# Results of the experts added in memory by the scatters of an MoE layer, after a differential attention and before and after a decaying attention

## Chip, cores and metric

One Trainium2 chip (trn2), one core. The metric is the device time of one execution in microseconds (us), median of 3 runs. TensorE is called PE below, VectorE DVE, ScalarE ACT, GpSimd POOL, SyncE SP. PE's clock has two levels, 1.2 and 2.4 GHz, and the profile gives the granted clock as a share of the upper one.

## What is computed

The input `x` holds 2 x 1024 tokens of 128 numbers. Four layers follow each other, each added to the residual; the second and the fourth are the same mixture of experts with the same weights:

```python
x = x + diff_attention(layernorm(x))      # 16 heads of 8
x = x + ffn(layernorm(x))                 # "m1" below
x = x + decay_attention(layernorm(x))     # 16 heads of 64
x = x + ffn(layernorm(x))                 # "m2" below

def ffn(x):
    scores = softmax(xf @ router_w.T)     # 8 experts
    topk_scores, topk_ids = top_k(scores, 2)
    topk_scores = topk_scores / topk_scores.sum(-1, keepdims=True)
    # each token: sum over its 2 experts of
    # score * ((silu(x @ w_gate) * (x @ w_up)) @ w_down), FF = 512
```

With two chosen experts the normalized scores are 1 / (1 + e) and e / (1 + e), where e is the exponential of the difference of the two logits.

## The kernel before

The residual `X` stays in SBUF as 128 partitions x 16 tiles x 128. `program` calls `diff_attention`, `moe` with tag m1, `decay_attention`, `moe` with tag m2, and the store of the output. Each is a block in which every engine has its own list of instructions in program order, tied by semaphores; blocks are separated by a barrier.

**In diff_attention** SP holds a list over 16 groups of heads (L533 to L549): `m_store(g)` stores the maxima of a group, and `load_operands(g + 2, ...)` loads the queries and keys of the group after next from DRAM, 24 transfers, once the second pass of PE is done with the group whose slot they take. PE computes the maxima of the groups ahead of the second pass; a transpose `turn` (L565) ends those of one group and those of the next begin.

**In moe** the routing comes first. PE counts tokens per expert (L1224, L1226) into `RC`, DVE turns the counts into places (`over` L1454 to `placeb` L1473), builds one-hot matrices in four passes over `c` (`marks`, `place_oh`, L1478 to L1483), and PE multiplies them into `IV`, from which DVE makes two lists: `source`, the token of each row, and `target`, the row where its result goes (L1494 to L1507). A slot is 128 rows for one expert; there are 39 slots, and 39 x 128 rows hold the 4096 results and some empty rows. ACT meanwhile normalizes `X` into `XN` (L1348), SP stores it as `xn_rows` in DRAM in four quarters (L1158). DVE takes the difference of the two best logits (`far`, L1485, L1486), ACT its exponential (L1351), which needs another table of functions, and then loads the table for Silu (L1354).

Then come the slots. POOL has this list: eight gathers ahead (L1196, `xs`, eight buffers), then for each slot s one gather for slot s + 8 and the scatter of slot s (L1202), which waits until DVE has copied the result from PSUM to `ys` (L1524, four buffers). PE turns a gathered tile (L1247), multiplies gate and up (L1256) and down (L1265); ACT copies weights (L1368) and takes Silu (L1362); DVE multiplies gate and up (L1517). The scatter writes first choices to rows 0 to 2047 of `yd_rows` and second choices to rows 2048 to 4095, and empty rows behind them.

Behind the slots `results_in` (L1147 to L1151) waits for all scatters, and SP and ACT load the first and the second results in four quarters each (`GB`, `gathered[q][k]`). ACT multiplies each tile of second results by its weight (`weigh`, L1387, 4 x 128x128 a quarter); DVE adds weight times first result to `X` (L1552, 4 x 128x128) and then the weighted second results (L1558, one of 128x512). In m1 the quarter goes on: statistics and mean (L1535, L1538) on DVE, the deviation on ACT (`deviations`, L1392), reciprocal and shift on DVE (`scales`, L1543, L1544), the normalized rows on ACT (`rows`, L1398), a transpose on PE and its copy on ACT (`turned_copy`, L1403). The last quarter's rows are made on DVE (L1568). PE runs products that nobody reads (L1300) in the waits: 26, then two for each weighed tile. In m2 SP stores the output in quarters (L2285), from the moment that the last quarter of first results has landed.

The constants of a layer are written by POOL at its start (L1178 to L1190); DVE waits for all eight of them (`const_r`) before `over`.

## Time and profile before

| what | value |
|---|---|
| median of 3 runs | 1128.02 us (1126.24 to 1129.11) |
| profiled execution: its time / its span | 1128.58 / 1126.8 us |
| PE, DVE, ACT, POOL busy | 1013.5, 749.7, 749.4, 438.6 us |
| granted clock of PE, mean | 0.956 |
| HBM read / written | 47.86 / 14.68 MB |

The span is the time from the first to the last instruction, and the execution's own time is 1.8 us more. Busy times are sums over layers that are bound by different things. m1 lies from about 492 to 653 us of the span, m2 from about 977 to the end.

### The profile page before, as it was taken

Reading aid. Unit: us, or ns where it says so; the run is one execution under the profiler, and the core shown is the slowest. Engines: PE = TensorE matmul, PEld = TensorE weight load, DVE = VectorE, ACT = ScalarE, POOL = GpSimd, SP = SyncE. Lnnn points to the kernel's source line nnn. Section 1 sums busy time; section 2 is a strip of 40 time slices with the busy share of each in tenths; the row PEclk is TensorE's granted clock in tenths of the full one; section 3 lists DMA queues with packets and bytes.
Section 4 is the critical chain, followed back from the end, with each engine's and each line's share of the span. In section 5 each row is a group of like instructions: output and inputs, shape, how many; then the busy total and the mean of one; then the engine's idle time right before and its main releaser. Section 6 shows DMA issues by size and latency. Waiting matters only on the chain. (4 is left out here: it accounts for less than half of the span.)

```text
span 1126.8 us, 26278 instructions
## 1 busy us (share of the span) xinstructions
PE 1013.5 (90%) x9920; PEld 696.6 (62%) x9920; DVE 749.7 (67%) x1513; ACT 749.4 (67%) x1513; POOL 438.6 (39%) x580
## 2 busy tenths in 40 slices
PE   5889999999999999758999889999999999489993
PEld 3333333333333334547999768787888888479993
DVE  6789999999999998882333545656565666443333
ACT  4658888888888887445666577675766666356663
POOL 3752112221121211216765134544444444257761
PEclk9889999999999999978999899999999999779997
DMA  2233111111111100611111421111111110021114
GB/s 71 88 111 114 31 30 43 46 31 30 30 36 45 39 2 2 222 41 46 48 48 37 160 71 76 38 76 38 77 38 76 39 74 3 10 62 50 48 41 126
DMA packets 40035, 64.67 MB, mean 57 GB/s; under 512 B 10025, under 2 KB 21033, under 8 KB 37993
## 3 DMA queue, kind: packets, MB, share of 16 engines
q1 hardware_dynamic: 31736, 50.14, 13.9%
q0 software_dynamic: 4992, 10.23, 3.4%
q10 hardware_dynamic: 3184, 2.63, 0.7%
q8 instruction: 82, 1.34, 0.5%
q14 instruction: 41, 0.33, 0.1%
HBM read 47.86 MB, written 14.68 MB: 56 GB/s over the span
## 5 line engine op out<-in xcount | busy, mean ns | idle before, releaser
L802 ACT ACTIVATE PB<-S 128x512 f32<-128x512 f32 x576 | 307.9, 597 | 71.0 <-PE S L608 66.2
L908 DVE TENSOR_REDUCE mx<-S 128x2 f32<-128x1024 f32 (+1 forms) x192 | 207.5, 1127 | 8.5 <-PE S L594 8.5
L870 POOL TENSOR_SCALAR_AFFINE_SELECT PB<-PB 128x512 f32<-128x512 f32 x128 | 79.3, 638 | 306.4 <-ACT PB L802 306.3
L643 PE MATMUL PV<-PB,VP 128*32 128x256 f32 (+2 forms) x2432 | 177.7, 379 | 0.0
L1517 DVE TENSOR_TENSOR m_hs<-m_gs,m_UP 128x512 f32<-128x512 f32 x78 | 53.7, 688 | 158.7 <-ACT m_gs L1362 156.6
L608 PE MATMUL S<-W 50*128 50x512 bf16 (+3 forms) x768 | 123.9, 328 | 4.9 <-ACT PB L802 4.2
L594 PE MATMUL S<-W 48*128 48x512 bf16 (+3 forms) x640 | 94.4, 326 | 13.1 <-DVE mx L904 4.9
L1202 POOL DMA_INDIRECT yd_rows<-m_ys,m_target x78 | 76.8, 984 | 58.9 <-DVE m_ys L1524 58.9
L1196 POOL DMA_INDIRECT m_xs<-xn_rows,m_source x78 | 76.0, 974 | 48.0 <-DVE m_source L1497 24.8
L643 PEld LDWEIGHTS PV<-PB,VP 128*32 128x32 f32 x2432 | 51.6, 108 | 69.1 <-issue 59.4
L594 PEld LDWEIGHTS S<-W 48*128 48x128 bf16 x640 | 26.8, 94 | 108.4 <-issue 43.1
L1256 PE MATMUL m_GP<-m_xt,m_wgu 128*128 128x128 f32 x624 | 84.5, 279 | 1.8 <-ACT m_xt L1358 1.8
L898 DVE TENSOR_REDUCE mx<-S 128x8 f32<-128x1024 f32 x64 | 78.3, 1223 | 10.8 <-PE S L587 10.1
L1256 PE MATMUL m_UP<-m_xt,m_wgu 128*128 128x128 f32 x624 | 83.9, 278 | 0.0
L1265 PE MATMUL m_YP<-W,m_hs 128*128 x624 | 82.6, 275 | 1.2 <-DVE m_ys L1524 1.2
L1368 ACT ACTIVATE m_wgu<-W 128x1024 f32 x78 | 82.6, 1058 | 1.4 <-issue 1.3
L1358 ACT ACTIVATE m_xt<-m_XT 128x128 f32<-128x128 f32 x78 | 21.7, 278 | 90.8 <-PE m_XT L1247 90.8
L1890 ACT ACTIVATE d_enegs<-d_PA 128x512 f32<-128x512 f32 x64 | 37.8, 591 | 64.7 <-PE d_PA L1684 60.2
L1256 PEld LDWEIGHTS m_GP<-m_xt,m_wgu 128*128 128x128 f32 x624 | 77.5, 195 | 2.9 <-issue 2.9
L1923 ACT ACTIVATE d_DM<-d_LQ,d_nL 128x128 f32<-128x128 f32 x252 | 78.1, 388 | 0.0
L1256 PEld LDWEIGHTS m_UP<-m_xt,m_wgu 128*128 128x128 f32 x624 | 77.6, 195 | 0.0
L1265 PEld LDWEIGHTS m_YP<-W,m_hs 128*128 128x128 f32 x624 | 75.8, 192 | 1.6 <-issue 1.6
(315 smaller groups left out, 1970.9 us busy)
## 6 DMA issues: line engine op xcount, KB each, us to landing
d_LQ<-l_rows SPq DMA_DIRECT2D x15, 1024.0 KB, 4.6
W<-qk_parts SPq DMA_DIRECT2D x210, 32.0 KB
qk_parts<-OT SPq DMA_DIRECT2D x24, 256.0 KB, 3.0
W<-qk_parts SPq DMA_DIRECT2D x30, 96.0 KB
W<-in_L_ffn_w_gate SPq DMA_DIRECT2D x1, 2048.0 KB, 10.0
W<-in_L_ffn_w_up SPq DMA_DIRECT2D x1, 2048.0 KB, 15.0
xn_rows<-m_XN SPq DMA_DIRECT2D x8, 256.0 KB, 2.3
m_GB<-yd_rows SPq DMA_DIRECT2D x8, 256.0 KB, 6.7
```

Source lines behind the costliest of these rows:

```text
L594: ins = nc.tensor.matmul(S1[:, b, a, 256 * k:256 * k + w], QS[base:base + KR, s, h, qb * P:(qb + 1) * P], KS[base:base + KR, s, h, c * 512 ...
L608: ins = nc.tensor.matmul(S2[:, j % 3, col:end], KS[base:base + KM, s, h, kb * P:(kb + 1) * P], QS[base:base + KM, s, h, q0:q0 + end - col] ...
L643: ins = nc.tensor.matmul(PV[32 * u:32 * u + 32, shift + col:shift + end], VP[:, g, kb, u // 2, :], PB[:, slot, col:end], start=(kb == 0 an ...
L802: nc.scalar.activation(PB[:, j % NPB, :], S2[:, j % 3, :], ACT.Exp, scale=SC).then_inc(exp_done, 1)
L870: nc.gpsimd.affine_select(out=tri, in_=tri, compare_op=ALU.is_ge, fill=0.0, base=0, pattern=[[0, U], [1, P]], channel_multiplier=-1).then_ ...
L898: nc.vector.reduce_max(mx[:, g % 2, 2].rearrange("p a h q -> p (a h) q")[:, :, q:q + 2], S1[:, b].rearrange("p a (h j k) -> p (a h) j k", ...
L908: nc.vector.reduce_max(mx[:, g % 2, c, :, heads[0], qb], S1[:, b, :, 0:w], AX.X)\
L1202: pool.indirect_dma_start(out=YD[:, :], out_offset=bass.IndirectOffsetOnAxis(ap=target[:, s:s + 1], axis=0), in_=ys[:, s % YB], in_offset= ...
L1256: last = nc.tensor.matmul(H[:, s % 2, j * P:(j + 1) * P], wgu[:, s % 2, k, j * P:(j + 1) * P], xt[:, s % 2], start=True, stop=True)
L1265: last = nc.tensor.matmul(YP[:, 0:P], hs[:, s % 2, j * P:(j + 1) * P], WD[:, bass.ds(e, 1), j, :].rearrange("p o d -> p (o d)"), start=(j ...
L1368: nc.scalar.activation(wgu[:, s % 2], W3[:, 0:2 * n].rearrange("p (k e f) -> p k e f", k=2, e=E) [:, :, bass.ds(e, 1), :].rearrange("p k o ...
L1923: last = nc.scalar.activation(DM[:, i, j % 2, j // 2], LQ[:, b, h], ACT.Exp, bias=nL[:, t, h:h + 1])
```

## The change

The weights of the choices are now in the table that is gathered: a row of `XN` and `xn_rows` has 130 numbers, the last two being 1 / (1 + e) and e. DVE takes a slot's weight from the gathered rows (`weight(s)`), and the copy out of PSUM multiplies by it. Each layer has its own result table. SP stores `X` into its first 2048 rows at the start of the layer, and SP writes zeros (7040 rows of 512 B) to all rows behind them during diff_attention, behind `m_store(2)` for m1 and `m_store(3)` for m2. The scatters add in memory (`compute_op=ALU.add`). Behind the slots one sum of the two loaded rows gives `X`; `weigh`, L1552 and the tile `wts` are gone. For this the exponential is taken ahead of `XN`: POOL computes `far`, ACT loads the table for Exp behind the first deviation, and the first quarter of `XN` is stored once the two extra columns are there. DVE waits for two constants before `over` and for all eight before `slotb`; in m2 it makes `rstd` and `shift` before the counts.

```diff
                     for g in range(1, G):
                         m_store(g)
+                        if g in (2, 3):
+                            clear_results(sp, "m1" if g == 2 else "m2")
...
-    XD, YD = scratch["xn"], scratch["yd"]
+    XD, YD = scratch["xn"], scratch["yd"][tag]
...
+        RW = P + 2
+        XNW = sb("XN", [P, NT, RW])
+        XN = XNW[:, :, 0:P]
...
             def _(sp):
+
+                sp.dma_start(YD[0:NTOK, :].rearrange("(p t) d -> p t d", t=NT), X[:]).then_inc(x_stored, 16)
                 for q in range(NQ):
                     sp.wait_ge(xn_ready, TQ * q + TQ)
-                    sp.dma_start(XD[q * TQ * P:(q + 1) * TQ * P, :].rearrange("(t p) d -> p t d", p=P), XN[:, quarter(q), :])\
+                    if q == 0:
+                        sp.wait_ge(table_ready, 1)
+                    sp.dma_start(XD[q * TQ * P:(q + 1) * TQ * P, :].rearrange("(t p) d -> p t d", p=P), XNW[:, quarter(q), :])\
...
                         pool.wait_ge(xt_done, s - XB + 1)
+                        pool.wait_ge(row_weighted, s - XB + 1)
...
                     pool.indirect_dma_start(out=YD[:, :], out_offset=bass.IndirectOffsetOnAxis(
-                        ap=target[:, s:s + 1], axis=0), in_=ys[:, s % YB], in_offset=None)\
+                        ap=target[:, s:s + 1], axis=0), in_=ys[:, s % YB], in_offset=None, compute_op=ALU.add)\
                         .then_inc(ys_stored[s % YB], 16)
 
+
+                nc.gpsimd.tensor_tensor(far[:], top[:, :, 1], top[:, :, 0], ALU.subtract).then_inc(apart, 1)
+                pool.wait_ge(apart, 1)
+                pool.wait_ge(rstd_ready, 1)
+                nc.gpsimd.tensor_tensor(far[:], far[:], rstd[:], ALU.mult).then_inc(far_ready, 1)
...
                 pool.wait_ge(targeted, 1)
+                pool.wait_ge(x_stored, 16)
+                pool.wait_ge(scratch["yd_zeroed"], 32)
                 for s in range(SLOTS):
                     if s + XB < SLOTS:
...
                     unread_products(26)
-                    for t in range(NT):
-                        pe.wait_ge(weighted, t + 1)
-                        unread_products(2)
+                    for q in range(NQ):
+                        pe.wait_ge(gathered[q][0], 16)
+                        unread_products(4)
...
                 nc.scalar.activation(sd[:, deviations_done:], mv[:, deviations_done:, 1], ACT.Sqrt, bias=norm["eps"][:])\
                   .then_inc(sd_ready, 1)
+
+                nc.scalar.activation(unread[:], norm["eps"][:], ACT.Exp)
+                act.wait_ge(far_ready, 1)
+                nc.scalar.activation(far_exp[:], far[:], ACT.Exp).then_inc(far_exp_ready, 1)
                 act.wait_ge(shift_ready, 1)
                 for t in range(NT):
                     nc.scalar.activation(XN[:, t, :], X[:, t, :], ACT.Identity, scale=rstd[:, t:t + 1],
                                          bias=shift[:, t:t + 1]).then_inc(xn_ready, 1)
-                act.wait_ge(far_ready, 1)
-                nc.scalar.activation(far_exp[:], far[:], ACT.Exp).then_inc(far_exp_ready, 1)
 
...
-                    for q in range(NQ):
-                        weigh(q)
...
-                    weigh(0)
-                    weigh(1)
-                    weigh(2)
                     deviations(0)
-                    weigh(3)
                     rows(0)
...
+                def scale():
+                    dve.wait_ge(sd_ready, 1)
+                    nc.vector.reciprocal(rstd[:], sd[:]).then_inc(rstd_ready, 1)
+                    dve.wait_ge(rstd_ready, 1)
+                    nc.vector.scalar_tensor_tensor(out=shift[:], in0=mv[:, :, 0], scalar=-1.0, in1=rstd[:], op0=ALU.mult,
+                                                   op1=ALU.mult).then_inc(shift_ready, 1)
+
+                if statistics_done == NT:
+                    scale()
+
+
                 dve.wait_ge(rc_done, 1)
-                dve.wait_ge(const_r, NCONST)
+                dve.wait_ge(const_r, 2)
                 total = RC[:, NT * E:(NT + 1) * E]
                 chain.link(nc.vector.tensor_tensor(over[:], total.unsqueeze(2).to_broadcast([P, E, NT]),
                                                    iot[:].unsqueeze(1).to_broadcast([P, E, NT]), ALU.is_gt))
                 chain.link(nc.vector.reduce_sum(tiles[:], over[:], AX.X))
-                dve.wait_ge(sd_ready, 1)
-                chain.link(nc.vector.reciprocal(rstd[:], sd[:]))
-                nc.vector.scalar_tensor_tensor(out=shift[:], in0=mv[:, :, 0], scalar=-1.0, in1=rstd[:], op0=ALU.mult,
-                                               op1=ALU.mult).then_inc(shift_ready, 1)
+                if statistics_done < NT:
+                    scale()
...
+                dve.wait_ge(const_r, NCONST)
                 nc.vector.tensor_copy(slotb[:].rearrange("p c i -> p (c i)"), sloti[:])
...
-                chain.link(nc.vector.tensor_tensor(far[:], top[:, :, 1], top[:, :, 0], ALU.subtract))
-                nc.vector.tensor_tensor(far[:], far[:], rstd[:], ALU.mult).then_inc(far_ready, 1)
+                    if m == 0:
+
+                        dve.wait_ge(far_exp_ready, 1)
+                        chain.link(nc.vector.tensor_scalar_add(far_sum[:], far_exp[:], 1.0))
+                        nc.vector.reciprocal(XNW[:, :, P], far_sum[:])
+                        nc.vector.tensor_copy(XNW[:, :, P + 1], far_exp[:]).then_inc(table_ready, 1)
...
-                dve.wait_ge(far_exp_ready, 1)
-                chain.link(nc.vector.tensor_scalar_add(far_sum[:], far_exp[:], 1.0))
-                chain.link(nc.vector.reciprocal(wts[:, 0], far_sum[:]))
-                chain.link(nc.vector.tensor_tensor(wts[:, 1], far_exp[:], wts[:, 0], ALU.mult))
+                chain.link(nc.vector.tensor_scalar(first_choice[:], iv[:, 2], -1.0, 1.0, ALU.mult, ALU.add))
+
+
+                def weight(s):
+                    dve.wait_ge(xs_loaded[s % XB], s // XB * 16 + 16)
+                    nc.vector.scalar_tensor_tensor(out=row_weight[:, s:s + 1], in0=xs[:, s % XB, P + 1:P + 2],
+                                                   scalar=first_choice[:, s:s + 1], in1=xs[:, s % XB, P:P + 1],
+                                                   op0=ALU.max, op1=ALU.mult).then_inc(row_weighted, 1)
...
-                    nc.vector.tensor_copy(ys[:, s % YB], YP[:, 0:P]).then_inc(y_copied, 1)
+                    dve.wait_ge(row_weighted, s + 1)
+                    nc.vector.tensor_scalar(ys[:, s % YB], YP[:, 0:P], row_weight[:, s:s + 1], None, ALU.mult).then_inc(y_copied, 1)
 
                 for s in range(SLOTS):
+                    weight(s)
                     gate(s)
                     if s:
                         y_copy(s - 1)
...
                     dve.wait_ge(xn_ready, NT)
                 for q in range(NQ):
                     dve.wait_ge(gathered[q][0], 16)
-                    for t in range(TQ * q, TQ * q + TQ):
-                        last = nc.vector.scalar_tensor_tensor(out=X[:, t, :], in0=GB[:, q, 0, t % TQ],
-                                                              scalar=wts[:, 0, t:t + 1], in1=X[:, t, :], op0=ALU.mult,
-                                                              op1=ALU.add)
-                    last.then_inc(first_added, 1)
-                    dve.wait_ge(weighted, TQ * q + TQ)
-                    dve.wait_ge(first_added, q + 1)
-                    nc.vector.tensor_tensor(X[:, quarter(q), :], X[:, quarter(q), :], GB[:, q, 1], ALU.add)\
+                    dve.wait_ge(gathered[q][1], 16)
+                    nc.vector.tensor_tensor(X[:, quarter(q), :], GB[:, q, 0], GB[:, q, 1], ALU.add)\
                       .then_inc(summed, 1)
                     if follow is not None:
...
+        def clear_results(sp, tag):
+            rows = scratch["yd"][tag][NT * P:, :].rearrange("(p k) d -> p k d", p=P)
+            sp.wait_ge(zeros_set, 1)
+            sp.dma_start(rows, zeros[:].unsqueeze(1).to_broadcast([P, NT + Router.SLOTS, P])).then_inc(yd_zeroed, 16)
```

How the instructions of three engines stand at three places, in program order; `x4` is a run of four, and line numbers with the change are those of the changed file. Start of m2 on ACT, before (L1344 is the deviation, `m_unread` a result that nobody reads, there to load a table):

```order
L1344 ACTIVATE norm_sd<-norm_mv,norm_eps 128x2
L1348 ACTIVATE m_XN<-X,m_shift,m_rstd 128x128 x16
L1351 ACT_TABLE_LOAD
L1351 ACTIVATE m_far_exp<-m_far 128x16
L1354 ACT_TABLE_LOAD
L1354 ACTIVATE m_unread<-m_far_exp 128x1
```

and with the change:

```order
L1361 ACTIVATE norm_sd<-norm_mv,norm_eps 128x2
L1364 ACT_TABLE_LOAD
L1364 ACTIVATE m_unread<-norm_eps 128x1
L1366 ACTIVATE m_far_exp<-m_far 128x16
L1369 ACTIVATE m_XN<-X,m_shift,m_rstd 128x128 x16
L1373 ACT_TABLE_LOAD
L1373 ACTIVATE m_unread<-m_far_exp 128x1
```

The exponential and its table stand ahead of the sixteen rows of `XN` instead of behind them.

DVE in m2, before: the end of the last of the four one-hot passes and what follows it.

```order
L1482 TENSOR_SCALAR m_marks<-m_marks,m_iop 128x312
L1483 TENSOR_TENSOR m_place_oh<-m_lane_no,m_placeb 128x1024
L1485 TENSOR_TENSOR m_far<-route_top 128x16
L1486 TENSOR_TENSOR m_far<-m_far,m_rstd 128x16
L1488 TENSOR_TENSOR m_sover<-m_ios,m_ends 1x312
L1490 TENSOR_REDUCE m_sef<-m_sover 1x39
L1491 TENSOR_SCALAR m_etab<-m_sef 1x39
```

With the change, DVE from the first pass to the second:

```order
L1495 TENSOR_TENSOR m_marks<-m_slot_no,m_slotb 128x312
L1497 TENSOR_TENSOR m_marks<-m_marks,m_tile_no 128x312
L1499 TENSOR_SCALAR m_marks<-m_marks,m_iop 128x312
L1500 TENSOR_TENSOR m_place_oh<-m_lane_no,m_placeb 128x1024
L1505 TENSOR_SCALAR m_far_sum<-m_far_exp 128x16
L1506 RECIPROCAL m_XN<-m_far_sum 128x16
L1507 COPY m_XN<-m_far_exp 128x16
L1495 TENSOR_TENSOR m_marks<-m_slot_no,m_slotb 128x312
L1497 TENSOR_TENSOR m_marks<-m_marks,m_tile_no 128x312
```

The three instructions of the table's columns (L1505 to L1507) stand between the first and the second pass, and the two of `far` are gone from DVE.

End of m1 on ACT, before (`m_GB` is the loaded results, `d_XNT` the copy of the turned rows):

```order
L1387 ACTIVATE m_GB<-m_GB,m_wts 128x128 x12
L1392 ACTIVATE norm_sd<-norm_mv,norm_eps 128x4
L1387 ACTIVATE m_GB<-m_GB,m_wts 128x128 x4
L1398 ACTIVATE m_XN<-X,m_shift,m_rstd 128x128 x4
L1392 ACTIVATE norm_sd<-norm_mv,norm_eps 128x4
L1398 ACTIVATE m_XN<-X,m_shift,m_rstd 128x128 x4
L1403 ACTIVATE d_XNT<-m_GP 128x512
L1392 ACTIVATE norm_sd<-norm_mv,norm_eps 128x4
L1398 ACTIVATE m_XN<-X,m_shift,m_rstd 128x128 x4
L1403 ACTIVATE d_XNT<-m_GP 128x512
L1392 ACTIVATE norm_sd<-norm_mv,norm_eps 128x4
L1403 ACTIVATE d_XNT<-m_GP 128x512 x2
```

and with the change:

```order
L1405 ACTIVATE norm_sd<-norm_mv,norm_eps 128x4
L1411 ACTIVATE m_XN<-X,m_shift,m_rstd 128x128 x4
L1405 ACTIVATE norm_sd<-norm_mv,norm_eps 128x4
L1411 ACTIVATE m_XN<-X,m_shift,m_rstd 128x128 x4
L1416 ACTIVATE d_XNT<-m_GP 128x512
L1405 ACTIVATE norm_sd<-norm_mv,norm_eps 128x4
L1411 ACTIVATE m_XN<-X,m_shift,m_rstd 128x128 x4
L1416 ACTIVATE d_XNT<-m_GP 128x512
L1405 ACTIVATE norm_sd<-norm_mv,norm_eps 128x4
L1416 ACTIVATE d_XNT<-m_GP 128x512 x2
```

The sixteen multiplications L1387 are gone, and the rest keeps its order.

## Rows read from the trace of the kernel before

**Rows 1.** The chain of waits over the whole execution, shares by engine and line
```profile
by line: PE m_GP L1256 3.2%; PE m_UP L1256 3.1%; PE m_YP L1265 3.0%; DMA m_GB<-yd_rows 0.6%; PE m_UP L1237 0.5%; PE m_XT L1247 0.4%; issue 0.3%; DMA m_xs<-xn_rows,m_source 0.2%; DMA yd_rows<-m_ys,m_target 0.2%; ACT m_GB L1387 0.1%; POOL m_l
```

**Rows 2.** Timeline of POOL in the slots of m2 (start us, us, engine, line, what, idle before)
```profile
1051.57 0.98 POOL L1196 DMA_INDIRECT m_xs<-xn_rows,m_source  x1 [0.30 <-issue]
1053.07 0.98 POOL L1202 DMA_INDIRECT yd_rows<-m_ys,m_target  x1 [0.52 <-DVE m_ys L1524]
1054.36 0.98 POOL L1196 DMA_INDIRECT m_xs<-xn_rows,m_source  x1 [0.30 <-issue]
```

**Rows 3.** DMA issues by line: count, median us from issue to landing
```profile
m_xs<-xn_rows,m_source POOLq DMA_INDIRECT x78, 2.6
yd_rows<-m_ys,m_target POOLq DMA_INDIRECT x78, 2.3
```

**Rows 4.** Timeline of the end of m1, all engines
```profile
633.17 0.69 DVE L1558 TENSOR_TENSOR X<-X,m_GB 128x512 f32<-128x512 f32 x1 [0.41 <-ACT m_GB L1387]
...
635.26 1.28 ACT L1387 ACTIVATE m_GB<-m_GB,m_wts 128x128 f32<-128x128 f32 x4 [2.12 <-DMA m_GB<-yd_rows]
...
637.86 0.33 SPq L2270 DMA_DIRECT2D d_WK<-in_L_attn_b_Wk  x1
637.98 0.28 ACT L1392 ACTIVATE norm_sd<-norm_mv,norm_eps 128x4 f32<-128x4 f32 x1
...
643.57 0.57 ACT L1403 ACTIVATE d_XNT<-m_GP 128x512 f32<-128x512 f32 x1
...
644.91 0.17 DVE L1543 RECIPROCAL m_rstd<-norm_sd 128x4 f32<-128x4 f32 x1
...
645.31 1.65 ACT L1398 ACTIVATE m_XN<-X,m_shift,m_rstd 128x128 f32<-128x128 f32 x4 [0.98 <-DVE m_shift L1544]
...
647.66 0.18 DVE L1543 RECIPROCAL m_rstd<-norm_sd 128x4 f32<-128x4 f32 x1 [1.18 <-ACT norm_sd L1392]
```

**Rows 5.** Timeline of the end of m2, all engines
```profile
1109.98 0.97 POOL L1202 DMA_INDIRECT yd_rows<-m_ys,m_target  x1 [0.78 <-DVE m_ys L1524]
...
1119.85 2.54 ACT L1387 ACTIVATE m_GB<-m_GB,m_wts 128x128 f32<-128x128 f32 x8 [0.68 <-DMA m_GB<-yd_rows]
...
1120.93 3.58 SPq L2285 DMA_DIRECT2D out_x<-X  x4
...
1123.41 0.69 DVE L1558 TENSOR_TENSOR X<-X,m_GB 128x512 f32<-128x512 f32 x1
```

**Rows 6.** Timeline of the start of m2, all engines
```profile
977.80 0.30 ACT L1344 ACTIVATE norm_sd<-norm_mv,norm_eps 128x2 f32<-128x2 f32 x1 [5.71 <-PEq L2281]
...
979.81 0.17 PE L1226 MATMUL m_UP<-route_M,m_tri 128*128 128x8 bf16 x1
...
981.37 0.29 DVE L1454 TENSOR_TENSOR m_over<-m_UP,m_iot 128x128 f32<-128x128 f32 x1 [4.57 <-POOL m_spare L1175]
...
982.01 0.25 DVE L1458 RECIPROCAL m_rstd<-norm_sd 128x16 f32<-128x16 f32 x1
...
993.49 0.17 DVE L1510 TENSOR_SCALAR m_far_sum<-m_far_exp 128x16 f32<-128x16 f32 x1
...
993.72 1.05 POOL L1196 DMA_INDIRECT m_xs<-xn_rows,m_source  x1 [12.46 <-DVE m_source L1497]
993.98 0.17 DVE L1512 TENSOR_TENSOR m_wts<-m_far_exp,m_wts 128x16 f32<-128x16 f32 x1
```

**Rows 7.** Timeline of the start of m1, DVE
```profile
496.03 0.29 DVE L1454 TENSOR_TENSOR m_over<-m_UP,m_iot 128x128 f32<-128x128 f32 x1 [0.68 <-POOL m_spare L1175]
```

**Rows 8.** The SyncE queue's timeline in attention, groups 2 and 3
```profile
118.98 2.44 SPq L529 DMA_DIRECT2D W<-mrow  x4
124.48 1.99 SPq L111 DMA_DIRECT2D W<-qk_parts  x6
```

**Rows 9.** Timeline of PE at the end of group 3's maxima
```profile
141.00 0.28 PE L565 MATMUL S<-ident,mxc 128*32 128x128 f32 x1
```

**Rows 10.** Stretch in which m1 stores XN: busy, PEclk, DMA share, GB/s
```profile
500.00:504.00 4.00, 3.16 (x15) 2.23 (x16) 3.90 (x12) 3.98 (x10) 0.00 (x0) 0.50 0.64 180
```

More of the change, by code:

```diff
@@ L1139, in moe @@
         ZP = XT[:, 0:NT * HE]
-        YTS = xs[:].rearrange("p b d -> p (b d)")
+        YTS = wgu[:, 0].rearrange("p k f -> p (k f)")
         NCONST = 8
@@ L2238, in _ @@
                 nc.gpsimd.memset(identb[:], 0.0).then_inc(ident_zero, 1)
+                nc.gpsimd.memset(zeros[:], 0.0).then_inc(zeros_set, 1)
                 nc.gpsimd.memset(norm["eps"][:], LN_EPS)
```

30 lines of the change are left out of this document (14 added, 16 removed).

## Prediction

> **What bounds the kernel.** I read the chain of waits first. It says which engine holds the end: PE in m2's slots (L1256, L1265) has most of what the answer covers, and two smaller entries bear on this change, the loads of results into `GB` (0.6%) and the two kinds of indirect transfers (0.2% each) [rows 1]. The slots are PE's: gathers start 2.79 us apart (1054.36 less 1051.57) all along, and only what lengthens that period, or what stands before and behind the 39 slots of a layer, can move the time. POOL is nearly full in a slot: a gather and a scatter, each 0.98 us with 0.30 us behind it, make 2.56 of 2.79 us, so 0.23 us are left [rows 2]. Then the timelines of four places: the two ends and the two starts of the MoE layers. Behind m1's slots, ACT and DVE work through quarters; the last quarter's reciprocal starts at 647.66 [rows 4], and all of decay_attention is behind it. Behind m2's slots the last quarter of results is there by 1121, while the last sum starts at 1123.41 [rows 5]. At m2's start DVE is idle for 4.57 us until POOL has written its last constant, and the first gather waits for DVE's list [rows 6].
>
> **End of m1.** Gone are 16 multiplications on ACT and 16 multiply-adds on DVE; the sum of a quarter (0.69 us) stays. What is late next? The second quarter is there at 635.26 (ACT's wait for it ends) and the last by 637.86, when SP, which waits for it, issues the next load [rows 4]. With the change the chain from 635.26 is: the sum, 0.69, and reciprocal with shift, 0.40 (644.91 to 645.31), so that ACT starts the rows of quarter 0 at 636.4. From there ACT and DVE alternate: three times rows of 1.65, three times a deviation of 0.28 and the 0.40 again (the last without the rows), and twice a copy of 0.57: 4.95 + 0.84 + 0.80 + 1.14 = 7.7, with some 0.05 for each of eight handoffs 8.1. The last reciprocal starts at 644.5 instead of 647.66: **-3.2 us**. DVE's sums and statistics (about 2.0 us a quarter) lie beside it, and the third and fourth quarters land before they are needed. What follows is unchanged work, if PE's clock holds.
>
> **End of m2.** ACT's last multiplications are released by a landing at 1119.85 and last 2.54 us for two quarters, so the last quarter has landed by 1121.1. One sum of 0.69 then ends at 1121.85, where it now ends at 1124.10. SP cannot start storing before 1120.93 in either kernel, and its 3.58 us for four stores hold waits for sums [rows 5]. Without them four issues of some 0.45 us end near 1122.6 instead of 1124.5: **-1.9 us**.
>
> **Start of m2.** DVE is released by the last matmul of the counts (979.81 + 0.17) instead of the last constant (981.37): -1.3. The reciprocal and what hangs on it (0.25 and its gap) go into the idle time behind the deviation of 977.80: -0.3. The two-column work comes in between the first and the second one-hot pass. The same three operations took from 993.49 to 994.15 before: +0.66. The first gather at 993.72 waited for DVE's `source`: **-1.0 us** [rows 6]. The rows of `XN` don't become the later wait: ACT's table load now stands in its idle time, the exponential is released by POOL behind its constants at about 981.75, and `XN` starts 0.4 us earlier than before; only its first quarter is stored 1 us later, behind the columns, and it isn't the last.
>
> **Start of m1.** The idle time before `over` is only 0.68 [rows 7], the columns cost 0.66, and the reciprocal stays in the chain: 0. `XN` starts about 0.3 us later behind the table load, and it has that room before the list.
>
> **In the slots.** `weight(s)` is one tiny DVE operation, and the copy becomes a multiplication, perhaps 0.05 us longer. DVE has nearly 2 us of each slot free, so 38 of 39 cost nothing; if the copy grew by over half a microsecond, PE would wait for it. The last one of a layer is exposed, as is one memset at the very start: +0.2 together.
>
> **The adding scatter** is in no row. Two prices. *Landing*: a plain scatter lands in 2.3 us, a gather, which reads DRAM, in 2.6 [rows 3]. Adding means reading the row, then writing. Lower bound 0, upper bound a whole gather in front, +2.6. Only the last scatter of a layer is exposed. I take +0.8, nearer to the low end, since the issue and completion inside those 2.6 are paid once; two layers: **+1.6 us**. The Trainium skill ("DMA: Bandwidth & Descriptors", Latency and other measured facts) gives an HBM access of 0.2 us on average; by that the term would be an estimated 0.4 and the sum 1.2 us lower. No row here shows it. *Issue on POOL*: lower bound 0, upper bound a second 0.98. I take +0.3, which exceeds the 0.23 us of slack by so little that four `ys` buffers absorb it (next part).
>
> **Traffic that is added.** SP writes 2 x 7040 rows of 512 B, 3.6 MB each, ahead of the loads of groups 4 and 5. The store of 512 B rows moved 180 GB/s at a DMA share of 0.64 [rows 10], so 280 GB/s at full share: 12.8 us. It starts when `m_store(2)` is issued (118.98 + 2.44 = 121.4), and is through by about 135.5. The loads that were issued from 124.48 land some 3 us behind it, near 139 [rows 8]. PE needs them when the maxima of group 3 are done, at 141.00 [rows 9]: hidden, with 2 to 3 us to spare, and the same pattern 23 us later for m2. The store of `X` (1 MB) lies ahead of the first `XN` store with 6 us of idle DMA. Rows of 520 B instead of 512 B: 0.
>
> **The sum.** -3.2 - 1.9 - 1.0 + 0.2 + 1.6 = -4.3. The profiled execution took 1128.58 us for a span of 1126.8; 1124.3 for one like it. The median of the runs is 0.56 lower, which gives **1123.7 us**, 0.4% below 1128.02. A measurement of this kernel can tell about 0.3% (3.4 us) from no change, so the line for faster is 1124.6.
>
> **Rivals.**
> - *POOL becomes the bound (slower).* If an adding scatter takes d longer to issue, POOL falls behind by d - 0.23 in each of the 31 slots that also have a gather. DVE needs the `ys` buffer four slots later: 4 x 2.79 = 11.2, less copy and handoff (0.6) and landing (3.1), leaves 7.5 us of lag, so it decides from d = 0.23 + 7.5 / 31 = 0.47. Above it each layer loses 31 x (d - 0.47); at d = 0.7 that is 7.1 us a layer and **1138 us**. At double the issue it would be 1155. For it: POOL's 0.98 us is the making of a list of transfers, and adding needs a second source. Against it: gather and scatter cost the same, though they differ in direction. A rule of the Trainium skill bears on it ("DMA: Bandwidth & Descriptors", SDMA does more than copy, and SWDGE vs HWDGE vs iDMA): addition there takes two streams, and POOL writes a descriptor pair for each copied row. Three descriptors instead of two would be an estimated d = 0.49, at the edge, and the time 1125.
> - *The gain is given back at the ends (no change).* Either the added read costs its upper bound (+3.6 more, 1127.3), or PE, which now has 16 unread products instead of 32 behind m1's slots and ACT's rows come in quarters between them, is at 1.2 GHz for the last transposes and the first products of decay_attention, which would return 2 to 3 us: about **1127 us**.
> - *Attention waits for its loads.* If writing zeros runs at the measured 180 GB/s instead of 280, it lasts 20 us, and the loads of groups 4 and 5 land near 144.5, 3.5 us late, twice: **1130.7 us**.
> - *The change does less than it says.* If the loads into `GB` land later, since four scatters that add are behind them in the memory, the quarters and not ACT set the end of m1; the saving then shrinks by as much. This is within the second case.
>
> **Chances.** Forecast 0.55 (of it 0.47 faster, 0.08 just short of the line, own range 1120.5 to 1126). Given back at the ends 0.19 (0.17 same, 0.02 slower). POOL 0.16 (0.03 same, 0.13 slower). Loads late 0.10, slower. Together faster 0.47, same 0.28, slower 0.25. The range reaches down to 1120, where landing costs nothing and the starts give a little more, and up to 1132, which holds late loads and a POOL bound of d up to 0.6; beyond it lies most of the POOL case, near 0.1, and some 0.05 lie below.
>
> **What the profile will show.** Right: POOL's scatter at most 1.4 us, gathers still 2.79 us apart in both layers, last reciprocal of m1 about 3 us earlier against the last scatter, one DVE operation of 0.69 per quarter in m2's end, `over` released by PE in m2, and no wait of PE for `qk_parts`. Wrong: DVE's multiplication waiting for `yd_rows`, a longer slot, a scatter landing beyond 4 us, or a granted clock below 1.00 from m1's last transposes on.

## The result, and the profile after the change

The changed kernel takes **1142.03 us** (median of 6 runs, 1140.07 to 1144.81), the kernel before 1128.57 us beside it (6 runs): ratio 1.0127, 95% interval 1.0108 to 1.0147. (The ratios here are taken over the fast runs and can differ a little from those of the medians, here 1.0119.) The prediction, 1123.7 us with a range of 1120 to 1132, was wrong in sign. The profiled execution took 1143.47 us for a span of 1141.6, so it is set against the 1126.8 of before: +14.8 us.

The table sets the same events of both traces side by side (start times in us, offset after less before). A stage costs what its offset has more than that of the line above.

| event | before | after | offset | the stage's own share |
|---|---|---|---|---|
| m1 begins (POOL's first fill) | 492.47 | 499.59 | +7.1 | attention **+7.1** |
| first gather of m1 | 508.45 | 514.89 | +6.4 | start -0.7 |
| last scatter of m1 | 625.04 | 638.51 | +13.5 | slots **+7.0** |
| loads into `GB` issued | 627.41 | 641.89 | +14.5 | last scatter **+1.0** |
| decay attention's first copy | 654.09 | 663.17 | +9.1 | end of m1 **-5.4** |
| m2 begins | 977.79 | 986.79 | +9.0 | decay attention -0.1 |
| first gather of m2 | 993.72 | 1001.41 | +7.7 | start -1.3 |
| last scatter of m2 | 1109.98 | 1124.00 | +14.0 | slots **+6.3** |
| loads into `GB` issued | 1112.35 | 1127.37 | +15.0 | last scatter **+1.0** |
| end of the span | 1126.8 | 1141.6 | +14.8 | end of m2 -0.2 |

Two things, the adding scatters and the place of the zeros, stand in the stages that cost 22 us, and the gains return 8.

**Slots.** The first fence is the timeline of POOL in m2 after the change, three scatters and two gathers in the middle and the last two (start us, us, engine, line, what, idle before). It answers to [rows 2].

```profile
1093.23 1.58 POOL L1212 DMA_INDIRECT yd_rows_m<-m_ys,m_target  x1 [0.30 <-issue]
1095.12 0.98 POOL L1206 DMA_INDIRECT m_xs<-xn_rows,m_source  x1 [0.31 <-issue]
1096.40 1.59 POOL L1212 DMA_INDIRECT yd_rows_m<-m_ys,m_target  x1 [0.30 <-issue]
1098.30 0.99 POOL L1206 DMA_INDIRECT m_xs<-xn_rows,m_source  x1 [0.30 <-issue]
1099.59 1.58 POOL L1212 DMA_INDIRECT yd_rows_m<-m_ys,m_target  x1 [0.30 <-issue]
...
1122.15 1.55 POOL L1212 DMA_INDIRECT yd_rows_m<-m_ys,m_target  x1 [0.30 <-DVE m_ys L1550]
1124.00 1.55 POOL L1212 DMA_INDIRECT yd_rows_m<-m_ys,m_target  x1 [0.31 <-issue]
```

A gather still takes 0.98 us, the adding scatter 1.58 instead of 0.98. With 0.30 behind each the pair takes 3.17 us (1096.40 less 1093.23) where PE's slot took 2.79, and nothing but 0.30 stands before any row: POOL has become the bound. The last scatters, without gathers between them, are 1.85 apart. Who feels it is DVE, whose multiplication writes a buffer that a scatter must have left (the waits of the window 1000:1130):

```profile
DVE m_ys L1550 <- DMA yd_rows_m<-m_ys,m_target: 10.3, 12, 1.1
```

**Attention.** The queue of SP around the first transfer of zeros, after the change, against [rows 8]:

```profile
119.18 2.44 SPq L529 DMA_DIRECT2D W<-mrow  x4
121.66 0.60 SPq L2264 DMA_DIRECT2D yd_rows_m<-zeros  x1
124.69 11.10 SPq L111 DMA_DIRECT2D W<-qk_parts  x6
135.83 1.05 SPq L115 DMA_DIRECT2D W<-qk_parts  x3
136.92 2.00 SPq L111 DMA_DIRECT2D W<-qk_parts  x6
```

Then PE, where it ran out of work, against [rows 9]. First the same place in the kernel before:

```profile
140.00 0.29 PE L594 MATMUL S<-W 48*128 48x128 bf16 x4
...
140.43 0.64 PE L643 MATMUL PV<-PB,VP 128*32 128x256 f32 x8
```

and after the change:

```profile
143.17 0.40 PE L596 MATMUL S<-W 48*128 48x128 bf16 x4 [2.90 <-DMA W<-qk_parts]
...
143.92 1.08 PE L645 MATMUL PV<-PB,VP 128*32 128x256 f32 x8
144.93 0.40 PE L567 MATMUL S<-ident,mxc 128*32 128x128 f32 x1
```

The transfer of zeros itself is issued in 0.60 us. The six loads behind it (a group has 18, not 24) take 11.10 us to be issued, in place of 1.99, of which the first alone takes 8.35. PE then waits 2.90 us for `W<-qk_parts` with four products of the next group's first maxima, and those stand *ahead* of the turn that I had read as the moment of need (L565 before, L567 now, at 144.93). The wait has a second price: PE's granted clock, 1.00 before it and at this place of the kernel before, is 0.50 (the lower level) from 142.3 to 149.2 us. It falls near the end of the 2.90 us in which PE stands still, and then eight products of L645 take 1.08 us in place of 0.64. That costs another 2.6 us: the product that starts at 149.12 is 5.7 us later than in the kernel before (143.38), and 0.2 of these were there ahead of the zeros. The second transfer does it again without the clock: SP's loads take 10.05 us from 152.52, and PE waits 0.70 us at 169.43. The turn of that group is 6.25 us late (170.44, before 164.19), and the last turn, near 430 us, still 6.2. The remaining 0.9 of the 7.1 arises behind that turn, at the end of attention, where the clock is at the lower level for another 3.4 us from 483.6, before not at all; what releases it I did not trace. Run 1 gives all of it back. The zeros landed in 15.0 us (DMA issues by line, median from issue to landing):

```profile
yd_rows_m<-zeros SPq DMA_DIRECT2D x2, 3520.0 KB, 15.0
...
xn_rows<-m_XN SPq DMA_DIRECT2D x8, 260.0 KB, 4.0
```

**Starts and ends.** After the change the start of m2 reads, against [rows 6]:

```profile
989.01 0.29 DVE L1472 TENSOR_TENSOR m_over<-m_UP,m_iot 128x128 f32<-128x128 f32 x1 [1.42 <-PE m_UP L1243]
...
993.31 0.17 DVE L1505 TENSOR_SCALAR m_far_sum<-m_far_exp 128x16 f32<-128x16 f32 x1
...
993.51 0.26 DVE L1506 RECIPROCAL m_XN<-m_far_sum 128x16 f32<-128x16 f32 x1
993.68 0.12 DVE L1507 COPY m_XN<-m_far_exp 128x16 f32<-128x16 f32 x1
...
1000.05 0.18 DVE L1518 TENSOR_SCALAR m_source<-m_token 128x39 uint32<-128x39 f32 x1
...
1001.41 1.06 POOL L1206 DMA_INDIRECT m_xs<-xn_rows,m_source  x1 [10.51 <-DMA xn_rows<-m_XN]
```

`over` follows PE, as forecast. The first gather, though, waits no longer for the list (ready at 1000.23) but for the store of the rows, of which a quarter now lands in 4.0 us, in place of 2.3 with rows of 512 B. The end of m1, against [rows 4] (the sums and the last reciprocal):

```profile
641.89 1.75 SPq L1156 DMA_DIRECT2D m_GB<-yd_rows_m  x4
...
646.35 0.69 DVE L1579 TENSOR_TENSOR X<-m_GB 128x512 f32<-128x512 f32 x1 [9.74 <-DMA m_GB<-yd_rows_m]
...
648.28 0.66 DVE L1579 TENSOR_TENSOR X<-m_GB 128x512 f32<-128x512 f32 x1
...
650.34 0.66 DVE L1579 TENSOR_TENSOR X<-m_GB 128x512 f32<-128x512 f32 x1
...
652.62 0.66 DVE L1579 TENSOR_TENSOR X<-m_GB 128x512 f32<-128x512 f32 x1
...
656.65 0.18 DVE L1570 RECIPROCAL m_rstd<-norm_sd 128x4 f32<-128x4 f32 x1 [1.19 <-ACT norm_sd L1405]
```

And the end of m2, against [rows 5]:

```profile
1127.37 1.76 SPq L1156 DMA_DIRECT2D m_GB<-yd_rows_m  x4
...
1131.78 0.69 DVE L1579 TENSOR_TENSOR X<-m_GB 128x512 f32<-128x512 f32 x1 [9.66 <-DMA m_GB<-yd_rows_m]
1133.38 0.69 DVE L1579 TENSOR_TENSOR X<-m_GB 128x512 f32<-128x512 f32 x1 [0.91 <-DMA m_GB<-yd_rows_m]
1135.19 1.50 DVE L1579 TENSOR_TENSOR X<-m_GB 128x512 f32<-128x512 f32 x2 [1.12 <-DMA m_GB<-yd_rows_m]
1135.75 2.31 SPq L2318 DMA_DIRECT2D out_x<-X  x4
```

### The profile page after: what moved, and what is told of

Its sections match the earlier page's. It is cut to its first block and busy times, and to the rows that moved or that the text cites. A ratio compares the mean times of both kernels' runs of the same rounds, so it can differ in the third digit from the quotient of the medians.

```text
span 1141.6 us, 26345 instructions
## 1 busy us (share of the span) xinstructions
PE 1023.4 (90%) x9904; PEld 698.6 (61%) x9904; DVE 758.1 (66%) x1557; ACT 739.7 (65%) x1483; POOL 486.0 (43%) x585
## 3 DMA queue, kind: packets, MB, share of 16 engines
q0 software_dynamic: 13728, 10.31, 7.1%
## 5 line engine op out<-in xcount | busy, mean ns | idle before, releaser
L645 PE MATMUL PV<-PB,VP 128*32 128x256 f32 (+2 forms) x2432 | 179.7, 382 | 0.0
L1212 POOL DMA_INDIRECT yd_rows_m<-m_ys,m_target x78 | 123.4, 1582 | 26.2 <-issue 20.1
L645 PEld LDWEIGHTS PV<-PB,VP 128*32 128x32 f32 x2432 | 51.8, 109 | 70.6 <-issue 61.6
L1273 PE MATMUL m_GP<-m_xt,m_wgu 128*128 128x128 f32 x624 | 87.0, 284 | 1.8 <-ACT m_xt L1377 1.8
L1387 ACT ACTIVATE m_wgu<-W 128x1024 f32 x78 | 82.6, 1058 | 3.9 <-DVE m_etab L1512 2.6
## 6 DMA issues: line engine op xcount, KB each, us to landing
W<-in_L_ffn_w_up SPq DMA_DIRECT2D x1, 2048.0 KB, 15.1
```

The source lines that it names most:

```text
L645: ins = nc.tensor.matmul(PV[32 * u:32 * u + 32, shift + col:shift + end], VP[:, g, kb, u // 2, :], PB[:, slot, col:end], start=(kb == 0 an ...
L1212: pool.indirect_dma_start(out=YD[:, :], out_offset=bass.IndirectOffsetOnAxis(ap=target[:, s:s + 1], axis=0), in_=ys[:, s % YB], in_offset= ...
L1273: last = nc.tensor.matmul(H[:, s % 2, j * P:(j + 1) * P], wgu[:, s % 2, k, j * P:(j + 1) * P], xt[:, s % 2], start=True, stop=True)
L1387: nc.scalar.activation(wgu[:, s % 2], W3[:, 0:2 * n].rearrange("p (k e f) -> p k e f", k=2, e=E) [:, :, bass.ds(e, 1), :].rearrange("p k o ...
```

## The experiments

My first theory for the whole: *POOL's issue price* makes the slots' loss, *the place of the zeros on SP's queue* makes attention's, and the rest of the change gains. The rivals: the landing and four buffers (slots), the added bytes themselves (attention), the weight's operation on DVE (slots), and gains that existed only because the rest was slow. The kernels ran on three chips, each beside the kernel before. On the first chip the kernel before itself takes 1182 us (the last section has what its traces show), so three of the four kernels of that chip were run again on the second, where it takes 1127.89; on the third (runs 2, 7 and 8) it takes 1127.09. Run 4 ran on the first chip alone.

**Run 1: zeros in pieces.** In place of the two transfers, behind `load_operands`:

```diff
+                        if 2 <= g < 12:
+                            clear_results(sp, "m1" if g < 7 else "m2", (g - 2) % 5)
```

with `[:, 11 * piece:11 * piece + 11]` of the rows in each.

> The changed kernel (1142.0 us) with the zeros of both tables written in ten pieces of 704 KB, one behind the loads of each of the groups 4 to 13, in place of two transfers of 3520 KB that stand ahead of the loads of groups 4 and 5. Theory A: the 7 us that the attention lost came from the two bursts, which held back SP's next loads (11.1 and 10.1 us to issue in place of 2.0) and with them PE at 143 us; in pieces behind the loads nothing waits: the first layer starts at 492 to 493 us in place of 499.6, and the time is 1135, 1134 to 1136.5. Theory B: the 7 MB cost the same wherever they are written, or the attention lost time to something else (the memset, the planner's order): the start stays at 497 to 500, the time above 1139.

Measured 1142.96 us where before took 1181.99; m1 begins at 490.43. The begin speaks for theory A, the time says nothing on that chip. Again on another:

> The changed kernel with its zeros in ten pieces, a second time: 1135, 1134 to 1136.5, where the changed kernel takes 1142; on the first call's chip the first layer started at 490.4 us in place of 499.6, but the first scatter of a layer came 14.8 us after its first gather in place of 12.2. If the pieces cost the second half of the attention what the bursts cost the first, it is above 1139.

Measured **1135.20 us** (before 1127.89 beside it, ratio 1.0071, 1.0043 to 1.0098). m1 begins at 492.98. The 7 us of attention were the bursts; 7 MB of zeros in ten pieces cost nothing that can be seen, and no product waits for `W<-qk_parts`. POOL's first to last scatter stays at 110.5 us in both layers.

**Run 2: is it the size or the place?** The two transfers whole, moved behind `load_operands` in the loop of SP:

```diff
                         m_store(g)
-                        if g in (2, 3):
-                            clear_results(sp, "m1" if g == 2 else "m2")
...
                             load_operands(sp, g + 2, (g + 2) % NQ)
+                        if g in (2, 3):
+                            clear_results(sp, "m1" if g == 2 else "m2")
```

> The changed kernel with its two transfers of zeros whole, as the change has them, but issued behind the loads of groups 4 and 5 in place of ahead of them. Theory A: the 7 us were a matter of place: SP's next loads could not be issued for 9 us behind a transfer of 7040 rows, and PE waited for them; behind the loads nothing is due on SP for 11 us (131.0 to 142.2 us), the two tiles' loads have been issued, and the first layer starts at 492 to 494: the time is 1135, 1134 to 1137, as with the pieces. Theory B: 3.5 MB at once take the transfer engines from the loads of group 4, which have just been issued, so these land late and PE waits as before: start at 496 to 500, time 1139 to 1142.

Measured 1136.72 us (before 1127.09 beside it, ratio 1.0082, 1.0062 to 1.0103), m1 begins at 490.02. Theory A. That m1 begins earlier than in the kernel before (492.47) is no gain: PE's turn that stands at 118.04 us in the trace before is already 2.8 us earlier here, and no zeros are written yet; the later turns keep these 2.8 up to 400 us. SP's queue in that run:

```profile
121.70 1.98 SPq L111 DMA_DIRECT2D W<-qk_parts  x6
...
127.96 0.61 SPq L2264 DMA_DIRECT2D yd_rows_m<-zeros  x1
139.16 3.18 SPq L529 DMA_DIRECT2D W<-mrow  x4
```

The same 3520 KB are issued at 127.96, behind the loads; the next item is due 11 us later and takes 3.18 us in place of 2.41. The loads of group 4, issued just ahead, were not late: PE's list of waits has no entry for `W<-qk_parts` left.

**Run 3: scatters that overwrite.** `compute_op=ALU.add` is taken away, the zeros stay as the change has them. The kernel leaves out the addition, so the residual is missing from its sums.

> The changed kernel with scatters that overwrite in place of adding; zeros, the store of the residual, weights at the copies and the sum of two rows stay. It leaves out the addition in memory. Theory A: POOL's issue of an adding scatter (1.59 us in place of 0.98) makes its cycle of a slot 3.18 us against the 2.79 of the other engines, and that and the last scatter's way are the whole +8.0 and +7.3 us of the slots: they fall to +0.3 or less, the cycle of POOL to 2.79, and the time is 1142.0 - 15.3 = 1127, 1126 to 1129. Theory B: what slows the slots is the weight's own operation on DVE and the gathers' wait for it: the cycle stays above 3 us, the time above 1135.

Measured 1186.37 us against 1181.99, with 130.6 and 133.0 us from first to last scatter: the stalls of that chip hide what a slot costs. Again:

> The changed kernel with scatters that overwrite, a second time, for the same reason as the first of this call; the addition in memory is left out. Theory A: 1127, 1126 to 1129 where the kernel before takes 1128 (with 104.3 us from first to last scatter in place of 110.4, the last scatter's start to the loads of results 2.4 in place of 3.4); the 7 us of the zeros' bursts stay. Theory B: the weight's operation on DVE and the gathers' wait for it also cost: above 108 us from first to last scatter, above 1133.

Measured **1126.97 us** (ratio 0.9995, 0.9975 to 1.0015). First to last scatter takes 104.39 us in each layer (before 104.33, changed kernel 110.51 and 110.39), last scatter to the loads of results 2.4 us. Theory A: the weight's operation on DVE, the wait of gathers for it, and the rows of 520 B add nothing to a slot. The adding alone is worth 15 us between the medians, 14.1 of them in the two stretches from the first scatter to the loads of results. The time stays above 1123 since the zeros' bursts are still in it: m1 begins at 497.09, and PE waits 2.2 and 0.8 us for `W<-qk_parts` and is at the lower clock behind the first for 3.4 us in place of 6.8. What this run does not give back is 0.8 of m1's +7.0: the first scatter is 13.1 us behind the first gather here and in the changed kernel, 12.3 before, 12.4 in run 1. The granted clock rises to 1.00 9.6 and 9.7 us behind the first gather in these two, 7.5 in the kernel before and 7.6 in run 1; so that part is slower products at the lower clock and not the adding.

**Run 4: eight buffers.** Zeros in pieces and `XB, YB = 8, 8`.

> The first kernel of this call (zeros in pieces) with 8 buffers of results for the scatters in place of 4. Theory A: POOL falls behind by 0.39 us a slot while gathers and scatters alternate (31 times, 12 us), with 4 buffers DVE has to wait for it and every engine with DVE; with 8 none waits, the last eight scatters, 1.85 us apart, catch up 0.9 us each, and 12.1 - 7.5 + 1.0 (landing) = 5 to 6 us remain of each layer's 8: the time is 4 to 5 us below the first kernel's, 1130 to 1132. Theory B: POOL's queue sets the end of the slots whatever is buffered ahead of it (its 39 scatters and 31 gathers run back to back from the third slot on): the same time as the first kernel's within 1 us. Theory C: DVE waited for the landings, not the issue: all 8 us go in both layers, 1120.

Measured 1142.43 us, and 1142.96 for run 1 on the same chip: theory B. (Theory A would have it 4 to 5 us below run 1.) DVE no longer waits for a buffer, and the end does not come sooner (the timeline of the end of m2's slots in this run):

```profile
1116.63 0.35 DVE L1550 TENSOR_SCALAR m_ys<-m_YP,m_row_weight 128x128 f32<-128x128 f32 x1 [1.45 <-PE m_YP L1282]
...
1122.79 1.55 POOL L1212 DMA_INDIRECT yd_rows_m<-m_ys,m_target  x1 [0.30 <-issue]
```

The last result is written at 1116.98, and the last scatter starts 5.8 us later. First to last scatter: 110.4 us, as with four buffers. What buffers change is who waits.

**Run 5: the change's other parts alone.** Scatters that overwrite one table, no zeros, no stored residual, and

```diff
-                    dve.wait_ge(gathered[q][1], 16)
-                    nc.vector.tensor_tensor(X[:, quarter(q), :], GB[:, q, 0], GB[:, q, 1], ALU.add)\
+                    nc.vector.tensor_tensor(X[:, quarter(q), :], X[:, quarter(q), :], GB[:, q, 0], ALU.add).then_inc(x_stored, 1)
+                    dve.wait_ge(gathered[q][1], 16)
+                    dve.wait_ge(x_stored, q + 1)
+                    nc.vector.tensor_tensor(X[:, quarter(q), :], X[:, quarter(q), :], GB[:, q, 1], ALU.add)\
```

> What the change has besides the addition in memory: rows of 520 B with the weights, the weight at the copy of a result, the exponential ahead of the rows, no work of ACT at a layer's end. Scatters overwrite one table for both layers, there are no zeros and no store of the residual, and DVE makes two plain sums of a quarter (0.7 us each) in place of four operations and one. It computes the reference in full. Theory A: it keeps the gains that the changed kernel shows (the end of the first layer -5.4 us, less 0.7 to 2 for the second sum, the layers' starts -0.7 and -1.3) and has none of its losses: 1128.6 - 6 = 1122.5, 1121 to 1125. Theory B: the gains of the ends came with the bursts and the later starts of the changed kernel (the loads of results ran emptier) and are gone with the sum of three: 1127 to 1129.

Measured 1182.62 against 1181.99 on the disturbed chip. Again:

> The kernel with the change's other parts and without the addition in memory, a second time: on the chip of the first call the kernel before itself took 1182 us where it had taken 1128.6, with ACT idle for 2 to 3.6 us at every third copy of a turned tile though the tile was there. Theory A: this belongs to that chip; where the kernel before takes 1128 this one takes 1121 to 1125, with 104.3 us from the first scatter to the last. Theory B: the gains at the ends are gone with the sum of three terms: within 2 us of the kernel before on whatever chip.

Measured **1123.72 us** against 1127.89, ratio 0.9971 (0.9957 to 0.9986): 0.3% faster than the kernel before, by the two ratios (0.9971 and 1.0127) 1.5% faster than the changed kernel, and it leaves nothing out. Theory A. By events: m1's first gather 15.5 us after its begin (before 16.0), last scatter to decay attention's first copy 25.4 (29.1), m2's first gather 14.7 after its begin (15.9), last scatter to the end 16.3 (16.8): -0.5, -3.6, -1.2, -0.5.

**Run 6: rows of 576 B**, `RW = P + 16` in run 5's kernel.

> The kernel before this in the list with rows of 144 numbers (576 B) in place of 130 (520 B) in the table of rows, and a fill of the 14 unused columns (0.2 us) on DVE. Theory A: rows whose length is no multiple of 64 B cost the store its time (4.0 us landing in place of 2.3 for 512 B): it falls to 2.3 to 2.8 and both layers start their gathers 1 to 1.7 us earlier, the time 2 to 3 us less. Theory B: the longer landing is the strided read of the store or its two packets a row: it stays at 4 us, the time within 0.5 us.

Measured 1123.89 us, the same as run 5. The store now lands in 3.1 us, and in m1 the first gather is released by the list again:

```profile
507.14 0.18 DVE L1513 TENSOR_SCALAR m_source<-m_token 128x39 uint32<-128x39 f32 x1
...
508.22 1.21 POOL L1202 DMA_INDIRECT m_xs<-xn_rows,m_source  x1 [11.29 <-DVE m_source L1513]
```

but 1.08 us behind the list in place of 1.24: in m1 the time was the list's within 0.2 us. In m2 the store still lands last, and the gather comes 1.43 us behind the list in place of 1.45. Neither theory is quite right: the row's length takes 1 of the 2 us of landing, and the time does not notice. Two packets a row are not it either: the whole kernel has 40036 packets with rows of 520 B and 40035 with rows of 512 B.

**Run 7: no wait before the output stores.** In m2, SP waits for the last load of first results before it looks at the stores:

```diff
-                sp.wait_ge(gathered[NQ - 1][0], 16)
+                if store is None:
+                    sp.wait_ge(gathered[NQ - 1][0], 16)
```

> The kernel of the change's other parts (1123.7 us) without SP's wait, in the second layer, for the last load of first results ahead of the stores of the output; each store still waits for its own quarter's sum. Theory A: the gain at the end of the second layer was given back there: SP holds the first store until 1115.5 us though the first quarter was summed at 1112.8, then issues four in 2.3 us and the last lands 3.2 to 3.5 us later in place of 2.3. Without the wait the last store is issued at the last sum's end, 0.8 us earlier, and lands in 2.3 to 2.6: 1.5 to 2 us less, from last scatter to end 14.5 to 15 us in place of 16.3. Theory B: the loads of results set the end and the output's landing is what it is: within 0.5 us of 16.3.

Measured 1122.56 us, ratio to before 0.9969 (0.9952 to 0.9986). Last scatter to end: 15.1 us in place of 16.3. The direction is theory A's, the size is 1.2 in place of 1.5 to 2, and the ratios of the two kernels (0.9969, 0.9971) cannot tell them apart; what shows the mechanism is the line of the stores, then that of the last sum:

```profile
1113.84 4.56 SPq L2315 DMA_DIRECT2D out_x<-X  x4
...
1117.31 0.69 DVE L1576 TENSOR_TENSOR X<-X,m_GB 128x512 f32<-128x512 f32 x1
```

The first store goes out when the first quarter is summed (1113.81), and the median landing of a store falls from 3.0 to 2.6 us.

**Run 8: those stores on two queues**, quarters 2 and 4 on ACT's.

> The same with the stores of the output shared by two queues, quarters 1 and 3 on SP's and 2 and 4 on ACT's. Theory A: with sums 1.6 us apart a store's issue (0.6 us) never waits for the one before it, so one queue is enough: the same as the kernel before it in this list within 0.5 us. Theory B: what a store waits for in its queue is the landing of the one before it: 0.5 to 1 us less.

Measured 1123.19 us (0.9965, 0.9954 to 0.9977); last scatter to end 15.3 us. Theory A: one queue is enough.

## Why the prediction was wrong, step by step

- **The adding scatter's issue, +0.3 taken, +0.60 measured** (0.98 to 1.58 us). The bounds (0 to 0.98) held it; the value did not. I took the low end since gather and scatter cost the same "though they differ in direction", which says nothing on a second source. The Trainium skill ("DMA: Bandwidth & Descriptors", SDMA does more than copy, and SWDGE vs HWDGE vs iDMA) has addition take two streams and POOL write a descriptor pair for a transfer; I worked an estimated 0.49 out of that, nearer than my own value and still short of the measured 0.60.
- **"Each layer loses 31 x (d - 0.47)"** (the rival; the forecast itself put the slots at nothing with the words "so little that four `ys` buffers absorb it") had a wrong step in it: that four buffers forgive 7.5 us of POOL's lag. They only postpone the moment when DVE feels it. The last scatter is an instruction of POOL, so POOL's own lag counts in full; what forgives is the tail, the last scatters without gathers. From the traces: first scatter to last gather 82.18 before and 94.23 after in m2 (+12.05, 31 slots of 0.39), last gather to last scatter 22.15 and 16.16 (-5.99): +6.1 a layer, where my formula gives 31 x 0.13 = 4.0. Run 4 shows the step itself wrong, run 3 that adding is the whole cause of these 6.1. With +0.8 and +0.3 between first gather and first scatter (the 0.8 not from adding, run 3) this is the +7.0 and +6.3 of the table.
- **Landing, +0.8 a layer.** From the last scatter's start to the loads it is 3.37 in place of 2.37: +1.0, of it 0.6 the issue. Landing itself cost 0.4, about half of what I took; run 3 gives the 2.4 back.
- **"Hidden, with 2 to 3 us to spare"** failed in three places. The zeros themselves were through when I had them, at 136.7 (forecast 135.5; the core moved 290 GB/s meanwhile, forecast 280). But I moved the loads' landing by the time that the zeros take on the transfer engines, and what grew was their *issue*, 11.1 us in place of 2.0, so that the group's last load landed at 143.03 and not near 139. The moment of need was read from the turn at 141.00, while a product of the next group's maxima stands ahead of it (L594 at 140.00 in the trace before). And a wait of PE was priced at its length, while behind this one the clock fell (2.90 us of waiting, 2.6 of slower products). The rival "attention waits for its loads" had the mechanism's name and chance 0.10. Its price, 3.5 us twice, is the measured 7.1 by luck: it came from slower zeros (180 GB/s), which were not slower, and it knew neither the issue nor the clock.
- **End of m1, -3.2, measured -5.4.** The chain from the second quarter's sum to the last reciprocal is 8.4 us (648.28 to 656.65), where I had 9.2; the rest is that DVE took up the second quarter sooner, 6.4 us behind the loads' issue in place of 7.7 (635.10 less 627.41). In the trace before it waited for a late landing; in the kernels with one sum its sum stands 1.93 us behind the first quarter's, whatever landed, and with two sums it starts 6.5 to 7.5 behind the issue. In m2 of the kernel before it is 6.1, so part of this 1.3 may be chance. Run 5 kept 3.6 of the 5.4 with a second sum.
- **End of m2, -1.9, measured -0.2.** The sums end at 1136.69, 2.4 us sooner behind the loads, where the forecast had 2.25. I had named the wait that holds the stores ("cannot start storing before 1120.93 in either kernel") and then forgot its other effect: four stores in 2.31 us end 1.4 us behind the last sum and land in 3.5 us, where spread ones landed in 2.3. Run 7 takes the wait away and gets 1.2 us.
- **Starts.** m2 -1.0, measured -1.3; m1 0, measured -0.7. The release by PE and the column operations went as written, and the clock did not charge for the unread products that are gone: decay attention has its 3.4 us at the lower level near its start in both kernels, and its length is the same within 0.1 us. "Rows of 520 B: 0" was nearly right for the time, not for the landing (4.0 us), which has become the last wait. Run 6 gains nothing; in single traces the store holds the first gather back by 0 to 0.9 us (it starts 0.8 to 0.9 us behind the end of the list where the list releases it, and 0.9 to 1.8 with rows of 520 B).
- **In the slots, 38 of 39 cost nothing:** right. The multiplication takes 0.35 us (0.28 before), the weight 0.21, and run 3 is at 104.39.

The forecast's sum had the right sign where the change moves work between engines and failed at both places where it adds transfers. The likeliest case was given 0.55, the POOL rival 0.16, and the two that came true together, in one mechanism each, were treated as if one excluded the other: POOL's 14.3 (at d = 0.7) and the loads' 7.0 on top of 1123.7 are 1145, far beyond the range that I gave.

## What to carry to other kernels

When the queue that issues transfers has 0.2 us of slack in a slot, its price for a new kind of transfer decides the change, and four more buffers ahead of it did not help here; compute what the queue needs from its first instruction to its last. Put a bulk transfer behind the loads that are due next on its queue, not ahead, and check what stands first in line for those loads. A wait that empties PE is longer than it looks when the clock falls behind it: read the products behind the wait too. When a chain gets shorter, look for the wait that is now in front of its last item.

## What the runs showed of the hardware

- An indirect scatter of 128 rows of 512 B occupies POOL for 0.98 us, one that adds in memory for 1.58, 1.55 to 1.65 us in its 78 cases; the packets of the software queue rise from 4992 to 13728 for the whole kernel, and are 4992 again in run 3. The queues' lines of the page, after the change (packets, MB, share of 16 engines):

```profile
q1 hardware_dynamic: 46136, 59.48, 16.5%
q0 software_dynamic: 13728, 10.31, 7.1%
```

- Behind a transfer of 7040 rows, issued in 0.6 us, the next small load on the same queue (SP), which is due 2.4 us later, holds the queue for 8.35 us in place of 0.27, and the five behind it another 1.0 more than before. With 11 us until the next item (run 2) the four small transfers there take 3.18 us in place of 2.4, and behind one of 1408 rows, also with 11 us (run 1), 2.41. A small one with something due at once was not tried, and whether the rows or the bytes of the large one hold the queue no run tells.
- A store of 512 rows, one of four of a table, lands in 2.3 us (median) with rows of 512 B, 4.0 to 4.5 with 520 B, 3.1 with 576 B.
- PE stood still for 2.90 us in attention, and near the end of this its granted clock fell to 0.50 for 6.8 us; behind 2.2 us in run 3 it fell for 3.4 us; behind 0.70 us it stayed at 1.00.
- **A chip on which overwriting is slow.** On the first chip the kernel before took 1176 to 1190 us, in 23 runs, and so did runs 3 and 5, all of which overwrite; the two adding kernels took 1143. ACT stood idle for up to 3.6 us at every second to third copy of a turned tile. From run 5's first trace, ACT and PE in one slot of m1:

```profile
530.15 0.28 ACT L1371 ACTIVATE m_xt<-m_XT 128x128 f32<-128x128 f32 x1 [1.08 <-PE m_XT L1258]
...
530.81 1.06 ACT L1381 ACTIVATE m_wgu<-W 128x1024 f32 x1
...
532.63 0.27 PE L1258 MATMUL m_XT<-ident,m_xs 128*128 128x128 f32 x1
...
534.52 0.28 ACT L1371 ACTIVATE m_xt<-m_XT 128x128 f32<-128x128 f32 x1 [2.66 <-DMA a_LQ<-in_L_attn_a_lk]
...
535.17 1.06 ACT L1381 ACTIVATE m_wgu<-W 128x1024 f32 x1
```

The tile is turned at 532.90 and the copy starts at 534.52; the trace blames a landing that has nothing to do with it, and the profile's chain has 3% for "another core or an unknown queue". The adding kernels on that chip show such a stall too (3.33 us of idle time before the copy at 1006.83 in run 1), but their slots wait for POOL anyway. In both layers of all four kernels there, first gather to first scatter took 14.6 to 14.8 us in place of some 12.2. Why a chip does this, and whether a bound POOL only covers the stalls or there are fewer of them, stays open (before the 39 copies of m1, ACT's idle time is put down to such a landing 11 times in run 5's first trace, 35.5 us in all, and once in run 1's, 3.3 us); the other chips showed none of it. The changed kernel itself was not run there, but with its zeros in pieces it measured 3.4% faster than before (0.9662, 0.9616 to 0.9707), where another chip has it 0.7% slower: a verdict from one chip can have the wrong sign.
